# A gated block on one Trainium2 core: quantisation with a padded minimum, loads in halves, and two value blocks projected inside the first feed-forward

## What is computed

```
s = jnp.clip(jnp.max(jnp.abs(xg), axis=-1, keepdims=True), EPS, None)
q = jnp.round(jnp.clip(xg * (QB / s), -QB, QB)) * (s / QB)
...
h = jax.nn.silu(_bitlinear(x, w1)) * _bitlinear(x, w2)
return _bitlinear(h, w3)
...
x = x + jnp.tanh(g_xattn[0]) * _L0_xattn_ref(_layernorm(x, axis=-1), ctx_2048, mask_BxS2_bk0)
x = x + jnp.tanh(g_ffn[0]) * _L0_ffn_ref(_layernorm(x, axis=-1), L0_ffn_w1, L0_ffn_w2, L0_ffn_w3)
x = x + jnp.tanh(g_xattn[1]) * _L1_xattn_ref(_layernorm(x, axis=-1), ctx_2048, mask_BxS2_ik0, ...)
x = x + jnp.tanh(g_ffn[1]) * _L1_ffn_ref(_layernorm(x, axis=-1), L1_ffn_w_gate, L1_ffn_w_up, L1_ffn_w_down)
```

## Time and profile before

| | |
|---|---|
| median of three runs | 260.58 us |
| the profiled execution's own time | 258.16 us |
| its span | 256.4 us |
| TensorE, VectorE, ScalarE, GpSimd busy, share of the span | 86%, 64%, 53%, 44% |
| mean granted TensorE clock | 0.96 |
| first attention, to the first `gate_up` | 0 to 44.09 us |
| first feed-forward, steps 0 and 1 | 44.09 to 65.83 us |
| its steps 2 to 6 | 65.83 to 107.14 us |
| step 7 and hand-over, to `q(1)` | 107.14 to 126.33 us |
| second attention and feed-forward | 126.33 to 256.4 us |

### The profile page before, as it was taken

How to read it: one execution, slowest core, us unless ns; L and a number is a source line. 1 busy time by engine, 2 the same in 40 slices (tenths; PEclk the granted TensorE clock), 3 DMA queues, 4 the chain that set the end, 5 groups by cost and what they waited for, 6 DMA issues and landing times. The chain is left out here.

```text
span 256.4 us, 5210 instructions
## 1 busy us (share of the span) xinstructions
...
## 2 busy tenths in 40 slices
...
DMA packets 9288, 12.59 MB, mean 49 GB/s; under 512 B 1072, under 2 KB 7984, under 8 KB 9264
## 3 DMA queue, kind: packets, MB, share of 16 engines
...
q10 hardware_dynamic: 432, 0.20, 0.3%
...
HBM read 11.22 MB, written 1.05 MB: 48 GB/s over the span
## 5 line engine op out<-in xcount | busy, mean ns | idle before, releaser
L1416 PE MATMUL PB<-SGN,WHI 128*128 128x512 f32 x128 | 40.5, 398 | 0.0
L768 DVE TENSOR_TENSOR QM<-SIL,PB 128x512 f32<-128x512 f32 x16 | 11.0, 688 | 31.7 <-ACT SIL L1102 31.7
L1219 PE MATMUL PB<-SGN,XQH 128*128 128x512 f32 x64 | 27.3, 426 | 2.5 <-DVE XQL L619 2.5
L315 POOL TENSOR_TENSOR RSTD<-MVS,MHALF 128x1 f32<-128x1 f32 x24 | 14.5, 603 | 32.4 <-DVE MVS L473 32.4
L1102 ACT ACTIVATE SIL<-PB 128x512 f32<-128x512 f32 x16 | 9.6, 599 | 34.8 <-PE PB L1416 34.8
L1433 PE MATMUL PB<-WHI,SGN 128*128 128x256 f32 x128 | 25.8, 284 | 1.4 <-DVE SGN L776 1.4
L1219 PE MATMUL PB<-SGN,XQL 128*128 128x512 f32 x64 | 26.6, 415 | 0.0
L1416 PEld LDWEIGHTS PB<-SGN,WHI 128*128 128x128 f32 x128 | 23.1, 188 | 4.2
L1416 PE MATMUL PB<-SGN,WLO 128*128 128x512 f32 x64 | 25.2, 394 | 0.0
L356 POOL TENSOR_TENSOR HBQ<-HBQ,HSD 128x512 f32<-128x512 f32 x16 | 16.7, 1046 | 17.6 <-ACT HBQ L1008 17.6
L1058 ACT ACTIVATE HBQ<-PB 128x512 f32<-128x512 f32 x32 | 17.5, 614 | 10.8 <-PE PB L1356 10.8
...
## 6 DMA issues: line engine op xcount, KB each, us to landing
...
```

The source lines that it names most:

```text
L315: nc.gpsimd.tensor_tensor(RSTD[:, bass.ds(t, 1)], MVS[:, bass.ds(t, 1), 1], MHALF[:], ALU.pow).then_inc(rstd_ready, 1)
L768: nc.vector.tensor_tensor(GU[:, b, :], SG[:, b, :], PB[2 * b + 1][:], ALU.mult).then_inc(d_g, 1)
L1219: mm = nc.tensor.matmul(PB[2 * half + m][:], part[:, p, c, :], sgn(m, c, a, b), start=(c == 0 and k == 0), stop=(c == DC - 1 and k == 1))
L1416: mm = nc.tensor.matmul(PB[2 * b + m][:], wcol(w_part, m, c, j), act_part[:, c, g * TG:(g + 1) * TG], start=(c == 0 and i == 0), stop=(c = ...
```

## The change

Seven things change together.

1. X, CTXT and CTX are loaded in halves of four tiles, first halves first; the small tensors come after the weights. The statistics of X's second half move behind the first tile's row maximum.
2. Of the eight projection blocks, two are done after tile 2 and none after tiles 6 and 7; the last two value blocks are done in step 0 of the feed-forward, one behind each `gate_up`. Value blocks are moved to SBUF by VectorE (`v_out`), key blocks by ScalarE.
3. Tiles 2 to 7 are normalised by GpSimd (`norm_a`) and no longer by VectorE in the first attention. For the feed-forward ScalarE normalises (`norm_x`, with scale and bias from GpSimd's `x_offset`) into XN.
4. The minimum 1e-5 is a 65th column of each group of XN and HB, so that the maximum over 65 columns holds it: `x_step` and `h_step` go. The factor 127 moves into `round_h`, into GpSimd's `x_factor` (four columns), and into the weight scales. GpSimd now also scales and unscales the rows of tiles 0 and 1.
5. `x_round` reads five groups of 64 from rows of 65 and writes 320 columns (before: 256 in place).
6. VectorE sums all of W0's sizes (eight slices of 512); ScalarE takes all signs, W3's too, in tiles 3 to 7. `down_scale` moves behind step 1's first `h_product`, the small constants of the second attention into steps 3 to 5, the normalisation of its tiles 0 and 1 into steps 6 and 7.
7. Tile 0's rows are transposed in step 7, `q(0)` comes right behind step 7, and ScalarE turns to `q_out(0)` and the exponentials' table before it rounds the last half. `hi_slice` 5 moves to the second feed-forward. Buffers are shared to make room (SM, EX, ET in QM; OT to D2 in HB).

```
-KV_PARTS = (("k", 0), ("k", 1), ("v", 0), ("k", 2), ("v", 1), ("k", 3), ("v", 2), ("v", 3))
-KV_AT = (1, 2, 3, 4, 5, 6, 7, 8)
+KV_PARTS = (("k", 0), ("v", 0), ("k", 1), ("k", 2), ("v", 1), ("k", 3), ("v", 2), ("v", 3))
+KV_AT = (1, 2, 2, 3, 4, 5, 16, 16)
+SIGN_AT = {3: (0, 1, 2), 4: (3, 4), 5: (5, 6), 6: (7, 8), 7: (9, 10, 11)}
+ABS_AT = {3: (0, 1), 4: (2, 3), 5: (4,), 6: (5, 6), 7: (7,)}
...
+            def norm_a(t, p):
+                pool.wait_ge(xt_done, t - 1)
+                pool.wait_ge(ln_done, t)
+                pool.wait_ge(rstd_ready, 1 if t < NT // 2 else 2)
+                nc.gpsimd.tensor_scalar(XH[:, p, :], X[:, t, :], MVS[:, t, 0:1],
+                                        RSTD[:, t:t + 1], ALU.subtract, ALU.mult
+                                        ).then_inc(ln_done, 1)
...
+                nc.vector.tensor_scalar(XW[:], XV[:, :, 0:GS], MAGIC, -MAGIC, ALU.add, ALU.add
                                         ).then_inc(b_xd, 1)
...
-                nc.vector.tensor_reduce(HSD[:, p, h_groups(half)],
-                                        h_part(p, half).rearrange("p (g s) -> p g s", s=GS),
+                nc.vector.tensor_reduce(HSD[:, p, h_groups(half)], HB[:, p, h_groups(half), :],
                                         AX.X, ALU.max, apply_absolute_value=True
                                         ).then_inc(b_am, 1)
 
-            def h_step(t, p, half):
...
+                if t == 0:
+                    v_out(6)
                 h_product(t, p, 1)
+                if t == 0:
+                    v_out(7)
...
+                nc.scalar.activation(XN[:, p, :, 0:GS],
+                                     X[:, t, :].rearrange("p (g s) -> p g s", s=GS), ACT.Identity,
+                                     bias=NMB[:, t:t + 1], scale=RSTD[:, t:t + 1]
+                                     ).then_inc(xn_done, 1)
...
-                nc.scalar.activation(h, h, ACT.Copy, bias=MAGIC).then_inc(b_w, 1)
+                nc.scalar.activation(h, h, ACT.Copy, bias=MAGIC, scale=QB).then_inc(b_w, 1)
```

More of the change, by code:

```diff
@@ L318, in _, with half_rstd @@
             pool.wait_ge(set_pool, 1)
-            for half in range(2):
+            def half_rstd(half):
                 ts = slice(half * NT // 2, (half + 1) * NT // 2)
@@ L325, in _ @@
+            half_rstd(0)
+            norm_a(2, 0)
+            norm_a(3, 1)
+            half_rstd(1)
+            pool.wait_ge(set_pad, 5)
+            for t in range(NT + 2):
+                step_a(t, t % 2)
             pool.wait_ge(ld["ident"], 16)
@@ L327, in _ @@
                 for half in range(2):
[L328 to L334 removed]
+                    spread_rows(c, half)
             def halves(buf, p, half):
@@ L348, in scale_h @@
                 pool.wait_ge(b_r, 2 * t + half + 1)
-                h = halves(HB, p, half)
+                h = h_part(p, half)
                 nc.gpsimd.tensor_tensor(h, h, spread(HR, p, half), ALU.mult).then_inc(b_v, 1)
@@ L492, in norm, with stats_half @@
                                         ).then_inc(ln_done, 1)
-            for half in range(2):
+            def stats_half(half):
                 ts = range(half * NT // 2, (half + 1) * NT // 2)
@@ L1088, in step_c @@
                     exp_c(t + 1, 1 - p, 3)
+            warm(ACT.Silu)
+            act.wait_ge(a_mk, NT)
+            act.wait_ge(wsc, 1)
+            pipeline(step_b, lag=0)
+            q_out(0)
             warm(ACT.Exp)
-            copy_ht(1, 1, 4, xt_done, c_q, c_ht, 2 * NT)
+            round_h(NT - 1, 1, 1)
+            hi_h(NT - 1, 0)
             for b in range(4):
                 exp_c(0, 0, b)
+            hi_h(NT - 1, 1)
+            copy_ht(1, 1, 4, xt_done, c_q, c_ht, 2 * NT)
             pipeline(step_c, lag=0)
@@ L1290, in q, with step_b @@
                 mm.then_inc(c_q, 1)
+            def step_b(t, p):
+                pe.wait_ge(b_xl, t + 1)
+                gate_up(t, p, 0)
+                if t == 0:
+                    kv(6)
+                    pe.wait_ge(wsc, 1)
+                if t == 1:
+                    pe.wait_ge(wsum3, 1)
+                    nc.tensor.matmul(PB[7][:, D:D + 1], ONES[:], ABSS[:, 2:3], start=True,
+                                     stop=True).then_inc(wsum3, 1)
+                if live(t - 1):
+                    transpose_hq(t - 1, 1 - p, 0)
+                if live(t + 1):
+                    transpose_xq(t + 1, 1 - p)
+                else:
+                    pe.wait_ge(b_xl, NT)
+                    xt_c(0, 0)
+                if live(t - 2):
+                    down_b(t - 2, 1)
+                gate_up(t, p, 1)
+                if t == 0:
+                    kv(7)
+                if live(t - 1):
+                    transpose_hq(t - 1, 1 - p, 1)
+                    down_b(t - 1, 0)
+            pipeline(step_b, lag=0)
             def head_sums(u, p):
@@ L1398, in _ @@
             scores(0, 0)
+            transpose_hq(NT - 1, 1, 1)
+            down_b(NT - 1, 0)
             down_b(NT - 1, 1)
```

557 lines of the change are left out of this document (275 added, 282 removed).

## The result

| | before | after |
|---|---|---|
| median, four runs each | 260.65 us (259.67 to 261.41) | 243.53 us (241.87 to 244.73) |
| the profiled execution | 258.16, span 256.4 | 244.73, span 242.9 |
| mean granted TensorE clock | 0.96 | 0.97 |

The ratio is 0.9341, 95% interval 0.9276 to 0.9405: faster by some 17 us. Ratios leave out executions more than 1.5% above the fastest of their kernel; the profiled executions of e4, e7 and e9 are of that sort, so only their order and waits are relied on.

What follows compares the result with a forecast made beforehand. VectorE was taken to pace the middle feed-forward steps, with waits and other limits elsewhere in the first 126.33 us. Gains 6.1 + 5.2 + 4.3 + 1.2 = 16.8 gave 241.4, plus 2.4 a median of 243.8 us; range 237.0 to 251.5.

Steps and rivals of the forecast that it cites:

- First attention: Stretch up to the first `gate_up`: forecast to come at 38.0 us instead of 44.09, a gain of 6.1 (4 to 8).
- I take the masking of the last tile at 35, as now: End of the first attention: last masking kept at 35 us, though the earlier start alone would give 33.
- that stood on this path: Two projection blocks of 1.65 to 1.75 us between last masking and first `gate_up`, forecast to come later or earlier instead.
- Steps 0 and 1: First to fifth `gate_up` of the first feed-forward: forecast to fall from 21.74 to 16.5 us, a gain of 5.2.
- both waits: TensorE's waits in the first two feed-forward steps, 2.52 us for XQL and 4.10 ahead of `down_b(0, 0)`, both forecast to go.
- The estimate of 1.0 for the clock: Allowance of 1.0 us for TensorE at the lower clock level behind the first `gate_up`; bounds nothing and about 3.
- Steps 2 to 6: Middle of the first feed-forward: TensorE paces, five steps of 7.4 us, 41.31 to 37.0, a gain of 4.3.
- in the microsecond per step that VectorE has to spare: First feed-forward: the constants moved to steps 3 to 5 and normalisations in 6 and 7 were forecast to fit VectorE's spare time.
- Hand-over: Step 7 up to `q(1)`: forecast to fall from 19.19 to 18.0 us, a gain of 1.2 (nothing to 2.5).
- Behind `q(1)`: Everything from `q(1)` to the end, some 130 us: forecast not to change.
- the padded rows: Rival: groups 65 apart break up GpSimd's reads and writes, a step 9.9 us, run 260.6 or more; chance 0.03.
- The rival of a step paced by the chain at 8.2: Feed-forward steps stay paced by chain, GpSimd or ScalarE at about 8.2 us, run 248.8; chance 0.22.

Runs made afterwards that it cites:

- e4: Changed kernel with ScalarE rounding the last half and casting ahead of `q_out(0)`, the exponentials' table loaded behind the last cast; ratio to the kernel before 0.959, median 250.85 us.
- e7: Changed kernel with `down_scale` back at the end of VectorE's step 1; ratio to the kernel before 0.964, median 251.96 us.
- e9: Changed kernel with CTXT and CTX loaded whole again, behind both halves of X; ratio to the kernel before 0.9499, median 247.47 us.
- e10: The changed kernel run again without an edit; ratio to the kernel before 0.9419, median 245.21 us.
- e1: Changed kernel with sums of W0's sizes, TensorE's sum and a rounding put behind the last masking; ratio to the kernel before 0.947, median 247.52 us.
- e3: Changed kernel with the last two value blocks back behind tiles 6 and 7 of the attention; ratio to the kernel before 0.9378, median 244.67 us.
- e5: Changed kernel with the minimum (`h_step`) again a VectorE instruction, twice a step; ratio to the kernel before 0.9501, median 248.22 us.
- e2: Changed kernel with the second attention's small constants in steps 5 to 7, not 3 to 5; ratio to the kernel before 0.9347, median 243.85 us.

## Why the prediction was right, and where its sum was not

243.8 was forecast and 243.53 measured, in the direction and by the mechanisms named. That they agree to 0.3 us is luck: the sum is less good than that. It said -16.8 against the profiled execution; between the two profiled executions the difference is 244.73 - 258.16 = -13.4. The medians lie 17.1 apart because the profiled execution of before stood 2.5 below its median and that of after 1.2 above its own. That this offset was carried as it was (2.4) was stated, but it is noise of an execution, not a property of the kernel.

Term by term (predicted, measured in after and in e10):

- *First attention*, -6.1; -3.5 and -2.1. This is the term that was mis-sized. The step that failed is "I take the masking of the last tile at 35, as now": it came at 37.12 (38.89 in e10), and the way from there to the first `gate_up` was 3.4 us (3.1 in e10), as forecast. Three things were wrong in it. The start gained some 0.9 by the halves (e9) and not 2. The six normalisations that left VectorE were priced by steps 2 to 6; in the attention they took 0.405 each (L490 above), 2.4 us in all and not 5, so VectorE's work up to the last masking grew (19.8 us between the first and the last, 18.1 before), and its sums and roundings stand ahead of the masking in program order (2.0 us by e1, of which at most 0.85 reach the first `gate_up`). And a block that comes earlier is not free: it lies ahead of the masking, in the stretch that grew by 1.87 us; this last is read from the windows and not tested. The other failing step is the two blocks "that stood on this path": e3 shows the move of the two into step 0 worth about 1 us at most, as one lay in the wait for the last exponential (1.64 us) and both come back in step 0.
- *Steps 0 and 1*, -5.2; -5.9 and -6.6. Right in both waits; e7 alone brings 2.98 us of the 4.10 back. The wait of 2.52 is gone too, but no run puts the constants and the normalisation back ahead of `lo_x(1)`, so its cause is argued from their order alone. The estimate of 1.0 for the clock lies within what was seen. From the first `gate_up` to the second the window is 4.49 us at a granted clock of 0.84 in after (first row), 3.81 at 1.00 in e10 (second) and 5.96 at 0.61 in e5 (third), whose edit touches nothing that TensorE waits for there: it is busy all the time in each.

```profile
40.56:45.05 4.49, 4.49 (x20) 3.72 (x20) 3.15 (x13) 3.83 (x8) 2.56 (x10) 0.84 0.98 347
```

```profile
41.96:45.77 3.81, 3.81 (x19) 3.19 (x19) 2.92 (x12) 3.75 (x8) 2.17 (x9) 1.00 0.90 295
...
40.44:46.40 5.96, 5.96 (x19) 4.80 (x20) 3.64 (x13) 4.14 (x9) 3.46 (x12) 0.61 0.92 347
```

  So the same work cost 0, 0.7 and 2.15 us more by the clock. By the rule that the prediction takes from the Trainium skill ("TensorE: Matmul & The Clock Gate", Part 1, on the HAM clock gate) an array that stood idle starts at half rate, which made it a whole `gate_up`, 1.9; e5 comes near that, after and e10 do not.
- *Steps 2 to 6*, -4.3; -4.8 and -4.8. The bound did pass to TensorE, and `x_round` (0.477), `norm_x` (0.604) and `x_factor` (0.203) cost what was estimated. Two errors nearly cancelled: the period was taken as 7.4 and is 6.93 and 7.02 in steps 2 and 3 (`transpose_xq` was added to a stretch that still held a wait of 0.2), and the constants, costed at nothing "in the microsecond per step that VectorE has to spare", took 1.4 (e2). That microsecond was an average over the step, but `x_absmax` behind them is in a chain.
- *Hand-over*, -1.2; -1.3 and -0.8. Right (though its own figures, 16.1 + 0.7 + 1.0, add up to 17.8 and not 18.0); e4 shows ScalarE's order carries it. My later reading of the trace, that this order costs, was wrong.
- *Behind `q(1)`*, 0; +1.9 and +0.3. The instructions are the same. The granted clock was 0.89 and 0.85 from 156.39 to 169.39 us in after; before had 1.00 in the mean of the whole stretch.

Of the rivals, the padded rows cost nothing: GpSimd's products take 1.046 and 1.044 us. By the rule on small read commands in the Trainium skill ("GPSIMD Engine Reference", Performance pitfalls for Q7 kernels) the prediction estimated 1.75; nothing like it shows for this form. The rival of a step paced by the chain at 8.2 came true in part, at 7.62 and 7.85 in two steps of five and by another cause, VectorE's constants (e2).
